# Cutting 125-row transfers into 112 and 13 rows in a graph layer kernel, and moving one load

## What is computed

```python
def layernorm(x):                      # over the last axis
    return (x - mean(x)) / sqrt(var(x) + 1e-5)

xn = layernorm(x)                      # x: [625, 1024] float32
# graph attention, 4 heads of 256
z  = einsum('ni,hif->nhf', xn, W)
el, er = (z * a_l).sum(-1), (z * a_r).sum(-1)
e  = leaky_relu(el[src] + er[dst], 0.2)
gnn = segment_softmax(e, dst) weighted sum of z[src] per dst
# linear attention, 16 heads of 64
q, k, v = split(xn @ w_qkv);  q, k = elu(q) + 1, elu(k) + 1
mix = (q @ (k.T @ v)) / (q @ k.sum(0)) @ w_o
x = x + gnn + mix
# ternary FFN
y = layernorm(x)
w_scale = mean(|weight|);  w_q = sign(weight) * (|weight| > 0.5 * w_scale)
i_scale = max(|y|) / 127;  y_q = clip(round(y / i_scale), -128, 127)
out = x + (y_q @ w_q.T) * w_scale * i_scale + bias
```

## Time and profile before

| | us |
|---|---|
| times of three runs | 494.27, 494.21, 491.24 (median 494.21) |
| span of the profiled execution | 491.9 |
| PE busy | 450.1 (92%) |
| DVE busy | 343.0 (70%) |
| ACT busy | 190.3 (39%) |
| POOL busy | 138.2 (28%) |
| DMA | 36.45 MB, mean 74 GB/s |

### The profile page before, as it was taken

One profiled execution on the slowest core, in us unless ns is written; L12 is line 12 of the kernel. 1 busy time (PEld: TensorE's weight loads), 2 busy tenths in 40 slices (PEclk: granted clock), 3 DMA queues, 4 the chain that ended last, 5 costly groups with the idle time before them and its releaser, 6 DMA issues.

```text
span 491.9 us, 8172 instructions
## 1 busy us (share of the span) xinstructions
PE 450.1 (92%) x2627; PEld 387.9 (79%) x2627; DVE 343.0 (70%) x905; ACT 190.3 (39%) x337; POOL 138.2 (28%) x105
## 2 busy tenths in 40 slices
PE   6549999998999899999999999999999999998891
PEld 4549989776778787779888887799999888887460
DVE  4468998897929777993157799536556478778751
ACT  2047654215254466336144644514442131112440
POOL 2041114262442422222232321147765000052100
PEclk9959999999999999999999999999999999999896
DMA  3534222122222212111122111136663011200032
GB/s 118 181 128 117 89 80 101 43 65 64 80 70 66 64 45 65 44 43 27 39 64 64 43 43 43 43 87 192 179 191 103 1 43 44 64 22 1 9 102 98
DMA packets 18750, 36.45 MB, mean 74 GB/s; under 512 B 2137, under 2 KB 2387, under 8 KB 18598
## 3 DMA queue, kind: packets, MB, share of 16 engines
q1 hardware_dynamic: 18723, 36.10, 24.1%
HBM read 33.54 MB, written 2.56 MB: 73 GB/s over the span
## 4 chain that ended last, share of the span: by engine, by line
PE 58%; DVE 20%; issue 7%; SPq 4%; DMA 4%; ACT 3%; DVEq 1%; ACTq 0%
PE ps L980 13%; PE ps L981 13%; PE ps L982 13%; PE ps L1007 7%; DMA f_raw<-in_ffn_weights 4%; PE ps L1232 4%; PE ps L1070 2%; PE ps L1102 2%; PE ps L1119 2%; DVE exp_a L743 2%; DVE score L724 2%; DVE junk L670 1%; DVE k_sb L713 1%; SPq L236 1%; DVE packed L634 1%
## 5 line engine op out<-in xcount | busy, mean ns | idle before, releaser
L296 POOL TENSOR_TENSOR w_lo<-w_raw,w_hi 128x512 fp32r<-128x512 f32 x52 | 73.3, 1413 | 192.6 <-ACT w_hi L336 192.6
L980 PE MATMUL ps<-w_hi,act_hi 128*125 128x512 f32 x240 | 96.7, 403 | 2.3 <-ACT tmp L409 2.2
L981 PE MATMUL ps<-w_lo,act_hi 128*125 128x512 f32 x240 | 94.6, 394 | 0.0
L982 PE MATMUL ps<-w_hi,act_lo 128*125 128x512 f32 x240 | 94.5, 394 | 0.0
L1007 PE MATMUL ps<-onehot_src,onehot_dst 125*125 125x314 bf16 x400 | 60.9, 313 | 16.3 <-DVE onehot_src L580 16.1
L1007 PEld LDWEIGHTS ps<-onehot_src,onehot_dst 125*125 125x125 bf16 x400 | 55.1, 144 | 21.5 <-DVE onehot_src L580 17.5
L336 ACT ACTIVATE w_hi<-w_raw 128x512 fp32r<-128x512 f32 x52 | 32.8, 633 | 84.4 <-PE ps L982 72.6
L980 PEld LDWEIGHTS ps<-w_hi,act_hi 128*125 128x125 f32 x240 | 44.5, 185 | 12.8 <-ACT tmp L409 2.6
L982 PEld LDWEIGHTS ps<-w_hi,act_lo 128*125 128x125 f32 x240 | 44.5, 185 | 11.3
L981 PEld LDWEIGHTS ps<-w_lo,act_hi 128*125 128x125 f32 x240 | 44.5, 185 | 9.9
L980 PE MATMUL ps<-act_hi,w_hi 128*128 128x312 f32 (+1 forms) x128 | 39.7, 310 | 0.0
(11 more groups left out here) (151 smaller groups left out, 873.0 us busy)
## 6 DMA issues: line engine op xcount, KB each, us to landing
w_raw<-in_weights SPq DMA_DIRECT2D x80, 256.0 KB, 2.7
f_raw<-in_ffn_weights SPq DMA_DIRECT2D x32, 256.0 KB, 2.8
x_sb<-in_x SPq DMA_DIRECT2D x5, 500.0 KB
out<-x_sb SPq DMA_DIRECT2D x9, 250.0 KB
alr<-in_a_lr SPq DMA_DIRECT2D x1, 1000.0 KB
bias_sb<-in_bias SPq DMA_DIRECT2D x1, 500.0 KB
out<-x_sb SPq DMA_DIRECT2D x2, 125.0 KB
edge_i<-in_edges SPq DMA_DIRECT2D x1, 78.1 KB
```

The source lines that it names most:

```text
L296: pool.tensor_tensor(w_lo[:, s, :], w_raw[:, s, :], w_hi[:, s, :].bitcast(f32), ALU.subtract).then_inc(w_ready, 1)
L980: pe.matmul(dst, a[0], b[0], start=first, stop=False)
L981: pe.matmul(dst, a[0], b[1], start=False, stop=False)
L982: return pe.matmul(dst, a[1], b[0], start=False, stop=last)
```

## The change

Every transfer whose tile has 125 rows is issued as two: rows 0 to 111, then rows 112 to 124 (P // 16 * 16 = 112). This holds for the edge lists, x, alr, bias and the stores. Both parts signal the same semaphore, so whoever waits now waits for 32. Transfers of 128 rows are as before. And alr is no longer loaded ahead of the first two FFN units but behind them.

```diff
         @block.sync
         def _(sp):
-            sp.dma_start(edge_i[:], edges.rearrange("a (p t) -> p a t", p=P)).then_inc(edges_in, 16)
+            CUTS = [(0, P // 16 * 16), (P // 16 * 16, P)]
+            for lo, hi in CUTS:
+                sp.dma_start(edge_i[lo:hi, :, :], edges.rearrange("a (p t) -> p a t", p=P)[lo:hi, :, :])\
+                  .then_inc(edges_in, 16)
             for t in range(NT):
-                sp.dma_start(x_sb[:, t, :], x[t * P:(t + 1) * P, :]).then_inc(x_in[t], 16)
+                for lo, hi in CUTS:
+                    sp.dma_start(x_sb[lo:hi, t, :], x[t * P + lo:t * P + hi, :]).then_inc(x_in[t], 16)
             for s in range(QUAD):
                 sp.dma_start(w_raw[:, s, :], weights[s]).then_inc(raw_in[s], 16)
-            sp.dma_start(alr[:], bass.AP(a_lr.tensor, 0, [[0, P], [1, 2 * D]])).then_inc(alr_in, 16)
...
             for s in range(2):
                 sp.dma_start(f_raw[:, s, :], ffn_weights[s]).then_inc(f_in[s], 16)
+            for lo, hi in CUTS:
+                sp.dma_start(alr[lo:hi, :, :], bass.AP(a_lr.tensor, 0, [[0, hi - lo], [D, 2], [1, D]])).then_inc(alr_in, 16)
...
-            sp.dma_start(bias_sb[:], bass.AP(bias.tensor, 0, [[0, P], [1, D]])).then_inc(bias_in, 16)
+            for lo, hi in CUTS:
+                sp.dma_start(bias_sb[lo:hi, :], bass.AP(bias.tensor, 0, [[0, hi - lo], [1, D]])).then_inc(bias_in, 16)
             for t in range(NT):
                 for i, (lo, hi) in enumerate(parts_of(t)):
                     sp.wait_ge(y_ready, 2 * t + i + 1)
-                    sp.dma_start(out[t * P:(t + 1) * P, lo:hi], x_sb[:, t, lo:hi]).then_inc(stored, 16)
-            sp.wait_ge(stored, 16 * (2 * NT + 1))
+                    for r0, r1 in CUTS:
+                        sp.dma_start(out[t * P + r0:t * P + r1, lo:hi], x_sb[r0:r1, t, lo:hi]).then_inc(stored, 16)
+            sp.wait_ge(stored, 2 * 16 * (2 * NT + 1))
...
-            pool.wait_ge(bias_in, 16)
+            pool.wait_ge(bias_in, 2 * 16)
...
-            dve.wait_ge(edges_in, 16)
+            dve.wait_ge(edges_in, 2 * 16)
...
-                            dve.wait_ge(x_in[a], 16)
+                            dve.wait_ge(x_in[a], 2 * 16)
...
-            dve.wait_ge(alr_in, 16)
+            dve.wait_ge(alr_in, 2 * 16)
```

## The result

| | before | changed |
|---|---|---|
| median of four runs, us | 493.21 (491.24 to 494.27) | 472.15 (470.98 to 472.26) |
| span of the profiled execution | 491.9 | 470.3 |
| PE busy | 450.1 (92%) | 448.4 (95%) |
| PE idle for DVE's one-hots (L1007, now L1015) | 16.3 | 5.4 |
| SP's last wait for the stores | 9.0 | 1.3 |

The changed kernel is faster by 4.4%: the ratio is 0.9562, 95% interval 0.9526 to 0.9598. Lines of the changed kernel are 8 higher than before from POOL's program on (L1007 is L1015).

The account below looks back on a forecast made before the run. PE bounds 116.8 to 481.5 us; outside it, 125-row transfers on five engines delay start and end. Start 14.5, bias 1.2 and stores 6.3 make 22.0 off span 491.9: 469.9, plus 2.3 gives 472.2 us, range 468 to 477.

Parts of the forecast that it names:

- Five engines for 125 rows, sixteen for 112: DMA: 125-row transfers use five of 16 engines, 112-row ones were taken to use 16, at 250 to 400 GB/s.
- First x tile at 5.5 to 6.2, saving 1.4 to 2.1: Start: the first x tile lands at 5.5 to 6.2 us, cutting DVE's 2.68 us wait by 1.4 to 2.1.
- Weight units at 15.5: Start: the last of the first four weight tiles lands at 15.5 us (12 to 18), where it was 26.
- End of segment 0 at 21.4, row 0's transposes at 21.9: Start: DVE ends segment 0's one-hots at 21.4 us, 1.0 added for POOL's collision; PE starts row 0's transposes at 21.9.
- One segment later, at 33.9: Start: PE's row 1 transposes come a 12.0 us segment later, at 33.9 instead of 48.42: 14.5 us earlier.
- From there on as before: After row 1's transposes PE and DVE work as before, so the start's gain passes whole to the PE-bound stretch.
- alr costs and brings nothing: Moving alr behind the FFN units: cost 0, and alone a gain of under 1 us.
- bias 1.2: Ahead of the last LayerNorm: cut bias lets POOL start and release DVE earlier, gaining 1.2 us (0 to 1.6).
- Stores 6.3: End: cut stores keep pace with y, leaving 4.1 us behind it instead of 10.4: 6.3 us less (5 to 7).
- No effect: Rival: the pair of transfers moves no faster than the one did; time 493.7 us, chance 0.05.
- the issue queue: Rival: SP's slow issues follow the number of transfers in flight, delaying the weight tiles; time 505 us, chance 0.04.
- Start half won: Rival: rate under 250 GB/s or ACT, DVE and POOL collide anew; up to 7 us lost, 477 to 481, chance 0.14.

Follow-up runs that it names:

- e7: Changed kernel with the cut at row 124 instead of 112 (pieces of 124 and 1 rows): 505.39 us, a single run.
- e5: Changed kernel with POOL's w_lo of the first four weight units moved to ahead of the last tile's act_lo, at about 60 us: 476.69 us.
- e8: Changed kernel with POOL's w_lo of the first four weight units moved behind all of its act_lo work: 471.15 us.
- e1: Changed kernel with bias and the stores again as single transfers of 125 rows, the loads of edge lists, x and alr still cut: 480.33 us.
- e2: Changed kernel with bias again one transfer of 125 rows, all else as changed: 473.26 us.
- e3: Changed kernel with alr, still cut, again ahead of the first two FFN units: 474.26 us.
- e9: As e8, and ACT does row tile 1 before the four weight splits, not behind them: 470.10 us.
- e12: As e9, with eleven matmuls on zeros on PE between its first and second pass over weight units: 468.97 us.
- e10: The changed kernel once more, unaltered (its repeat), on the same chip as e8 and e9: 472.63 us.
- e4: Kernel before with only the load of alr moved behind the first two FFN units, transfers whole: 492.5 us against 493.42.
- e6: Changed kernel with eight matmuls on zeros put into PE's idle gaps in segment 1: 473.19 us.
- e11: The kernel before once more, unaltered (its repeat): span of the profiled execution 491.2 us.

## Why the prediction was right, point by point

The forecast was 472.2 us, the median is 472.15. That nearness is luck in part: of its three terms one was 3.6 us too large, and two others and one that it did not have made it up.

- *Five engines for 125 rows, sixteen for 112.* Right: share 1.04 at 4 to 16 us; e7 shows the divisor at work. The rate, 268 to 314 GB/s, lies between the bounds of 250 and 400.
- *First x tile at 5.5 to 6.2, saving 1.4 to 2.1.* Right: 6.03, saving 1.5. *Weight units at 15.5.* ACT had the first at 14.41 and splits at full speed from there. Right.
- *End of segment 0 at 21.4, row 0's transposes at 21.9.* 22.0 and 22.8. POOL's hold cost 3.7 us, not 3; e5 and e8, without it, have row 0's transposes at 20.2 and 19.8. Right in kind, 0.9 short. "Its clock still up" holds in the first profile and not in the repeat, where it is 0.50 from 20 to 26 us and row 0 comes at 24.5.
- *One segment later, at 33.9.* This is the step that failed: "A segment of sixteen edge tiles in the steady part is 60.39 - 48.42 = 12.0 us". The steady segment is PE's: it has several tiles in the ring ahead of it, and in the kernel before it runs through all 80 matmuls (the line below) although act_lo holds two of DVE's one-hots there too. In segment 1 PE is close behind DVE, and the hold by POOL's act_lo of row 0 reaches it: 13.90 to 13.98 us in seven kernels (e1, e2, e3, e5, e8, e9, e12) with the clock at 1.00, and 15.6 in the changed kernel's profile with the clock's fall besides. That act_lo is the reason is read from PE's waits; no run moved it. The kernel before could have warned: its own segment 1 takes 13.0 to 13.2 us (35.28 to 48.42), not 12.0. Row 1 came at 38.3 and 37.2; the term was 10.1 to 10.9 us, not 14.5.

```profile
49.31 11.24 PE L1007 MATMUL ps<-onehot_src,onehot_dst 125*125 125x314 bf16 x80
```

- *From there on as before.* Right: 37.4 us from row 1's transposes to the end of counting in e1, e2, e3 and e10 as in before, and 36.6 in the changed kernel's first profile.
- *alr costs and brings nothing.* Right (e3, e4).
- *bias 1.2.* By time 1.1 to 1.9 (e2), within overlapping intervals; by DVE's rows 1.3 (4.0 less 2.7). Right as far as can be told. The hazard named beside it ("may also strike DVE's attention rows of tile 4") is real, but its bound was wrong: the text let it eat the 1.6 us at most, and where it strikes it costs some 4 to 5 us (e12, e6).
- *Stores 6.3.* 7.1 by time (e1 against e2), 7.5 to 7.7 in the profiles of e1, before and changed, but 5.3 between the two repeats. Mis-sized was the last store: from the last y to the end 2.7 us, not 4.1, since the wait is 1.3.
- *Not in the sum.* The FFN took 1.7 us less, its clock at 1.00; that this comes from the change is not shown.
- *The rivals.* "No effect" fell with the share, "the issue queue" with 0.42 us an issue. "Start half won" was the nearest to what happened at the start (10.1 to 10.9 of 14.5), by a collision of DVE and POOL, though not the one over row 1's square root.

## What to carry to other kernels

Look at the DMA share while one kind of transfer is alone in flight: here 0.32 of sixteen engines was a row count that splits into five, and cutting off the odd rows cost one issue of about 0.4 us. Where a late transfer goes away, ask what the engine that waited for it will now collide with; here GpSimd's operations met VectorE's and took back some 3 of the 14 us by which the counting can end sooner (e8 against e10), and in the times moving them to where VectorE is idle brought 1.5 us, within the noise. A segment's duration may be carried over to another place only if the engine that sets the pace has the same lead there.

## What the runs showed that was not expected

- GpSimd's elementwise operations do not slow VectorE in proportion: a VectorE operation that meets one waits it out, however small it is itself (0.16 us became 2.39 beside an addition of 2.34, 0.36 became 1.3 beside one of 1.26). This was seen with the one-hots and with operations on two inputs, not with the one-input operations on 125x1 (0.14 to 0.15 throughout). In the 10.4 us of GpSimd without a break in e5 VectorE made nine one-hots, four and a half edge tiles; at 0.57 us a tile it makes eighteen alone.
- The changed kernel has a knife edge that the kernel before lacks: 0.5 to 0.8 us between two tiny operations of the last but one LayerNorm and POOL's first addition, where it was 2.4 before, and 4 to 5 us when both operations are met.
- TensorE's clock fell to its lower level behind idle times of 1.1 to 2.7 us in some executions and not in others of the same program: behind the same wait of 2.2 us it is 0.50 at 117 us in e11 and 1.00 in the first profile of before; at the start it is 0.50 from 20 to 26 us in e10, behind gaps of 1.73 and 1.65 us, and 1.00 in e1, behind gaps of 1.37 and 1.64. Each fall cost 1.6 to 2.1 us. Part of the spread between the timed runs of one kernel goes with it: in e12 the mean granted clock is 0.999 to 1.000 in the four runs of 468.4 to 469.0 us and 0.996 in those of 470.3 and 470.8.
